# Layer 1 of a graph network on one core: three picked groups a turn, re-ordered steps, and a turned one-hot that is read with a stride

## What is computed

```
e_in     = concat(x[src], x[dst])                     # 200000 x 256
edge_new = relu(e_in @ We1 + be1) @ We2 + be2
agg      = segment_sum(edge_new, dst)                 # 6250 x 128
x        = layernorm(x + x + relu(concat(x, agg) @ Wn1 + bn1) @ Wn2 + bn2)
```

## Time and profile before

| | |
|---|---|
| median of three runs | 4093.22 us |
| profiled execution, its own time | 4090.99 us |
| its span | 4088.8 us |
| mean granted TensorE clock | 0.844 of 2.4 GHz |
| layer 1, first gather to the end | 2179.3 to 4088.8 us |
| PE, DVE, ACT, POOL busy, whole span | 2902.8, 2493.5, 2497.4, 2964.7 us |

### The profile page before, as it was taken

How to read it: one execution, slowest core, us unless ns; L and a number is a source line. 1 busy time by engine, 2 the same in 40 slices (tenths; PEclk the granted TensorE clock), 3 DMA queues, 4 the chain that set the end, 5 groups by cost and what they waited for, 6 DMA issues and landing times. The chain is left out here.

```text
span 4088.8 us, 90253 instructions
## 1 busy us (share of the span) xinstructions
PE 2902.8 (71%) x18890; PEld 2648.6 (65%) x18891; DVE 2493.5 (61%) x5568; ACT 2497.4 (61%) x10068; POOL 2964.7 (73%) x3137
## 2 busy tenths in 40 slices
PE   6888888888888788888865565655556565666656
PEld 4877777777777777777744555555556555555656
DVE  4877777777777777777765444444444555555544
ACT  3767777777777677777646555455555555555553
POOL 5777777777777777777536777777777777777775
PEclk8999999999999999999987777767767777777777
DMA  6333333333333333333234333333333333333332
GB/s 190 81 81 81 83 81 81 81 82 81 82 80 82 81 84 81 81 81 83 57 108 108 95 90 94 94 91 94 90 94 94 93 99 94 98 97 95 97 99 63
DMA packets 426429, 367.97 MB, mean 90 GB/s; under 512 B 276875, under 2 KB 355163, under 8 KB 426108
## 3 DMA queue, kind: packets, MB, share of 16 engines
q0 software_dynamic: 98240, 214.20, 20.4%
q1 hardware_dynamic: 316720, 143.31, 14.0%
q10 hardware_dynamic: 11214, 8.17, 0.7%
HBM read 343.89 MB, written 21.44 MB: 89 GB/s over the span
## 5 line engine op out<-in xcount | busy, mean ns | idle before, releaser
L724 POOL DMA_INDIRECT he<-h_table,src_i x1563 | 1480.7, 947 | 514.9 <-issue 504.3
L1744 POOL DMA_INDIRECT msg<-p_table,src x1507 | 1422.3, 944 | 467.1 <-issue 461.6
L1777 PE MATMUL p_sumT<-msg,hot 128*80 128x129 f32 x3136 | 595.7, 369 | 688.2 <-ACT sumT L1830 683.7
L1777 PEld LDWEIGHTS p_sumT<-msg,hot 128*80 128x80 f32 x3136 | 542.5, 215 | 725.4 <-issue 533.9
L1622 ACT COPY picked<-hT 128x1 f32 x7168 | 759.9, 187 | 412.4 <-issue 398.3
L1762 PE MATMUL p_edge<-r_win,hotT 80*128 80x128 f32 x3136 | 480.0, 312 | 59.7 <-DVE msg L1899 45.8
L763 PE MATMUL p_score<-qk_two,heT 128*128 128x160 f32 x1568 | 396.7, 336 | 165.4 <-ACT heT L873 163.4
L1762 PEld LDWEIGHTS p_edge<-r_win,hotT 80*128 80x128 f32 x3136 | 452.6, 227 | 63.7 <-issue 63.2
L1899 DVE TENSOR_TENSOR msg<-msg,p_edge 128x512 f32<-128x512 f32 x392 | 243.6, 662 | 377.5 <-DMA msg<-p_table,src 376.4
L765 PE MATMUL p_score<-qk_win,heT 128*128 128x80 f32 x3136 | 465.2, 273 | 0.0
L765 PEld LDWEIGHTS p_score<-qk_win,heT 128*128 128x128 f32 x3136 | 454.3, 200 | 0.0
(11 more groups left out here) (210 smaller groups left out, 4565.5 us busy)
## 6 DMA issues: line engine op xcount, KB each, us to landing
dst_row<-in_dst_dram SPq DMA_DIRECT2D x196, 320.0 KB
feat<-in_edge_attr_dram SPq DMA_DIRECT2D x196, 128.0 KB
he<-h_table,src_i POOLq DMA_INDIRECT x1563
msg<-p_table,src POOLq DMA_INDIRECT x1507
qk_win<-qk_table SPq DMA_DIRECT2D x196, 40.0 KB
qk_two<-qk_table SPq DMA_DIRECT2D x392, 20.0 KB
r_win<-r_table SPq DMA_DIRECT2D x196, 40.0 KB
qk_table<-qk SPq DMA_DIRECT2D x13, 512.0 KB
```

The lines of the kernel that those rows point to most:

```text
L724: e.indirect_dma_start(out=he[u][:, j, 2 * FE:2 * FE + ROW], out_offset=None, in_=h_table[:, :], in_offset=bass.IndirectOffsetOnAxis(ap=sr ...
L1744: e.indirect_dma_start(out=msg[u][:, j, 0:D], out_offset=None, in_=p_table[:, :], in_offset=bass.IndirectOffsetOnAxis(ap=src_i[u][:, j:j + ...
L1777: mm = e.matmul(p_sumT[:, :], hot_of(c)[:, j, :], msg[u][:, j, 0:D + 1], start=(j == 0), stop=(j == J - 1))
```

## The change

- `PICKED` is (5, 0, 3). Chunks 5 and 3 are picked by ACT, 128 columns each, chunk 0 by DVE (`tensor_copy`), 128 columns. `group_of` gives None for the two groups other than 5 in turn 0, so these chunks gather all eight columns there; from turn 1 on they are picked a turn ahead. `pick_first` is gone. `pick_step` spreads ACT's 256 columns over seven steps (37 each), DVE's 128 over the first five (26 each). The node numbers go to registers in up to 16 at a time.
- `hotT` keeps the order in which `dst_row` was loaded. Its one operation compares with the node's number plus the window's start, worked out once for all chunks (`node_b`), with no second operand. `column` gives TensorE every eighth number (every seventh in a picked chunk, after the first 128) as the weights.
- Steps: PE does `edges` of the next chunk, `turn_back` of the one before, `sums` of its own (before: `sums` of the one before, `turn_back` of two before, `edges` of the next). ACT does `copy_sums` of the one before, its relu, then the picks (before: picks, `copy_sums` of two before, relu). DVE does the one-hots of the next chunk, `add` of two before, the picks, `boths` (before: `boths`, then `add`). Below, the three `step` functions stand in this order.

```
-PICKED = (5, 1)
-BATCH = 8
-BY_ACT = P // BATCH
+PICKED = (5, 0, 3)
+BY_ACT = (P, 0, P)
+BY_DVE = tuple(P - n for n in BY_ACT)
+AT_ONCE = 16
...
-            hotTs = [sb(f"hotT{k}", [W, J, P], ctx=ctx) for k in range(2)]
+            hotTs = [sb(f"hotT{k}", [W, CH], ctx=ctx) for k in range(2)]
...
                     def group_of(c):
-                        return PICKED.index(c[1]) if at_first and c[1] in PICKED else None
+                        g = PICKED.index(c[1]) if at_first and c[1] in PICKED else None
+                        return None if g and isinstance(c[0], int) and c[0] == 0 else g
...
+                        start = first + (0 if of is BY_ACT else BY_ACT[g])
+                        parts = -(-n // AT_ONCE)
+                        ends = [start + n * k // parts for k in range(parts + 1)]
+                        for at, to in zip(ends, ends[1:]):
...
                             i, u = c
-                            if u == 2 and not (isinstance(i, int) and i == 0):
+                            if u == 0 and not (isinstance(i, int) and i == 0):
+                                load_picks(2, i)
+                            elif u == 3 and not (isinstance(i, int) and i == 0):
                                 load_picks(0, i)
-                            elif u == 5 and not (isinstance(i, int) and i == TURNS - 1):
+                            elif u == 4 and not (isinstance(i, int) and i == TURNS - 1):
                                 load_picks(1, i + 1)
...
+                        def column(c, j):
+                            flat = hotT_of(c)
+                            if is_last(c):
+                                return flat[:, j * P:(j + 1) * P]
+                            if group_of(c) is None:
+                                return flat[:, :].rearrange("w (p j) -> w j p", j=J)[:, j, :]
+                            if j == 0:
+                                return flat[:, 0:P]
+                            return flat[:, P:CH].rearrange("w (p j) -> w j p", j=J - 1)[:, j - 1, :]
...
                         def step(c):
-                            if not is_first(c):
-                                sums(shift(c, -1))
-                            if not is_first(c) and not is_first(shift(c, -1)):
-                                turn_back(shift(c, -2))
                             if not is_last(c):
                                 edges(shift(c, 1))
+                            if not is_first(c):
+                                turn_back(shift(c, -1))
+                            sums(c)
...
-                        def step(c):
+                        def step(c, k=None):
+                            if not is_first(c):
+                                copy_sums(shift(c, -1))
+                            relus(c)
+                            if k is not None and c[1] == 4:
+                                relu_hidden(e, k)
                             if at_first:
                                 pick_step(e, mybir.EngineType.Activation, e.copy, picked_act, c, BY_ACT)
-                            if not is_first(c) and not is_first(shift(c, -1)):
-                                copy_sums(shift(c, -2))
-                            relus(c)
...
+                            e.tensor_scalar(hotT_of(c)[:, :], dst_row[u][:, :], node_b[:, bass.ds(number(c), 1)], None,
+                                            ALU.is_equal).then_inc(hotT_done, 1)
...
                         def step(c):
                             if not is_last(c):
                                 hots(shift(c, 1))
-                            boths(c)
                             if not is_first(c) and not is_first(shift(c, -1)):
                                 add(shift(c, -2))
+                            if at_first:
+                                pick_step(e, mybir.EngineType.DVE, e.tensor_copy, picked_dve, c, BY_DVE)
+                            boths(c)
```

More of the change, by code:

```diff
@@ L1475, in gnn_kernel, with made @@
             picked_act = sem("picked_act")
-            def pick_number(g, turn):
-                return turn * len(PICKED) + (g - 1) % len(PICKED)
+            picked_dve = sem("picked_dve")
+            def made(of, g, turn):
+                each = sum(n > 0 for n in of)
+                upto = sum(n > 0 for n in of[0:g + 1])
+                return turn * each + (upto + each if g == 0 else upto)
             in_win_done = sem("in_win_done")
@@ L1620, in pick_columns @@
                                 skip_runtime_bounds_check_because="the source of an edge is the number of a node")
-                            for k in range(BATCH):
+                            for k in range(to - at):
                                 op = copy(picked[g][:, at + k:at + k + 1], x1T[:, bass.ds(nodes[k], 1)])
-                        if first + n == of:
+                        if first + n == of[g]:
                             op.then_inc(done, 1)
                     def pick_step(e, engine, copy, done, c, of):
-                        per = -(-len(PICKED) * of // SLOTS)
@@ L1638, in pick_first @@
-                    def pick_first(e, engine, copy, done, of):
-                        pick_columns(e, engine, copy, done, 1, 0, 0, of, of)
+                        per = -(-sum(of) // (SLOTS if of is BY_ACT else SLOTS - 2))
+                        at, end = c[1] * per, min((c[1] + 1) * per, sum(of))
+                        for g in range(len(of)):
+                            low = sum(of[0:g])
+                            first, n = max(at - low, 0), min(end - low, of[g]) - max(at - low, 0)
+                            turn = c[0] if g == 0 else c[0] + 1
+                            if n > 0 and not (isinstance(turn, int) and turn == TURNS):
+                                pick_columns(e, engine, copy, done, g, turn, first, n, of)
@@ L1659, in load_picks @@
                             if not isinstance(turn, int) or turn > 0:
-                                before = val(e, pick_number(g, turn) - len(PICKED) + 1)
-                                e.wait_ge(picked_act, before)
-                                e.sem_inc(passed, 1)
+                                for done, of in ((picked_act, BY_ACT), (picked_dve, BY_DVE)):
+                                    if of[g]:
+                                        e.wait_ge(done, val(e, made(of, g, turn - 1)))
+                                        e.sem_inc(passed, 1)
                             at = val(e, (turn * SLOTS + PICKED[g]) * CH)
@@ L1713, in _ @@
                         if at_first:
-                            for g in (1, 0):
-                                load_picks(g, 0)
+                            load_picks(0, 0)
                         for u in range(1, SLOTS):
@@ L1933, in step_grouped @@
                                 normal(e, k)
+                        e.tensor_scalar(node_b[:, :], start_b[0:W, :], node_c[:, 0:1], None, ALU.add).then_inc(fixed, 1)
+                        e.wait_ge(fixed, val(e, FIXED + 1 + r))
                         hots((0, 0))
                         if at_first:
+                            e.sem_inc(picked_dve, sum(n > 0 for n in BY_DVE))
                             e.sem_inc(y_done, 1)
```

57 lines of the change are left out of this document (20 added, 37 removed).

## The result

The changed kernel took 4568.52 us (median of 4 runs, 4564.85 to 4571.53) against 4095.76 (4 runs): a ratio of 1.1156 [1.1137, 1.1175]. It is slower by 11.6%, where 4062 and a gain of 0.8% were forecast. Its profiled execution took 4566.30 us with a span of 4564.6, that is 475.8 us more than the span of before.

What follows compares the result with a forecast made beforehand. POOL's queue of layer 1 gathers was taken as the bound: first gather 2179.3, plus 1847.9 to the last, plus 29.1 less 1.5 to the end, plus 5 for POOL, 2.2 around the span: 4062 us, range 4050 to 4096.

Steps and rivals of the forecast that it cites:

- Picks on ACT: ACT's 256 picked columns a turn: 0.162 us each with loads, 41 us a turn; larger batches at worst the same time.
- Picks on DVE: DVE's new 128 columns a turn, ahead of boths: 0.162 us each (0.06 to 0.24), 20.7 us a turn, 0 on the path.
- Rival D: DVE becomes the bound above 0.288 us a column; at 0.35 a turn is 74 us, some 4280 us; chance 0.04.
- Order of the steps: New step order on PE, ACT and DVE: hidden by POOL in steady state, 1.5 us won at the end (0 to 2.4).
- POOL beside DVE: New DVE work from SBUF to SBUF beside POOL's gathers: costs 5 us, bounds 0 and 27 us.
- rival B: The gathers get longer: 22 ns a gather eats the whole gain, 4091 us; chance 0.11.
- Rival C: A gather stands still while DVE runs a one-hot: 188 us minus 34, 4245 us; chance 0.03.
- Fewer gathers: POOL's gathers in layer 1 fall from 1507 to 1481, 26 less at 1.2486 us: 32.5 us off the path.
- The turned one-hot: DVE's one-hot falls from 2.08 us a chunk to 1.27 (lower end half of that); 0 on the path.
- TensorE reads it strided: TensorE's 16 strided weight loads a chunk take 1.61 times as long, 1.41 us more; 0 on the path under POOL.

Runs made afterwards that it cites:

- a1: The changed kernel with each batch of node numbers starting at a column that is a multiple of four: 4108.17 us, ratio 1.0017 to the kernel before.
- b1: The kernel before with its list of picks shifted by one number, so no batch of eight starts at a multiple of four: 4974.53 us, ratio 1.2132.
- a2: The changed kernel with DVE's add after boths again, batches still unaligned: 4334.59 us, ratio 1.0572 to the kernel before.
- a7: The changed kernel with batches starting at multiples of four and the turned one-hot's second operand in PSUM, still contiguous: 4111.61 us, ratio 1.0039 to the kernel before.
- a8: The changed kernel with batches at multiples of four, the one-hot's second operand in PSUM and DVE's add after boths: 4058.98 us, ratio 0.9909 to the kernel before.
- c3: a8 with the old order of steps on TensorE and ACT: 4230.62 us, ratio 1.0328 to the kernel before.
- c1: a8 with the old layout of the turned one-hot (DVE strided, TensorE's weights contiguous): 4060.04 us, ratio 0.9901 to the kernel before.
- b3: The kernel before with strided weights alone (one-hot contiguous, its second operand in PSUM): 4139.31 us, ratio 1.0107.
- b2: The kernel before with only the new one-hot from SBUF to SBUF and the strided weights: 4154.72 us, ratio 1.0145.

## Why the prediction was wrong

**The steps that failed first are "Picks on ACT" and "Picks on DVE".** They took 0.162 us a column on both engines and said of larger batches "at worst the same time". Measured: 0.240 and 0.290. The price of a register load was scaled with its length from one row of eight numbers; that the row held only batches from multiples of eight was not seen, and the change splits 37 columns of ACT's step in three and DVE's 26 in two. The upper end for DVE, 0.24, rested on the same row. Undoing this alone (a1) brings 4568 to 4108, and doing it alone (b1) brings 4101 to 4975. With aligned batches, the column costs 0.143 and 0.193: the form of the term was right.

**Rival D named half of the place, and was mis-sized.** It had a chance of 0.04, from 0.288 us a column on, and at 0.35 a turn of 74 us and 4280 us. DVE measured 0.290 with the ring and 0.252 without it (a2). Without the ring the turn is (4263.0 - 2185.5) / 28 = 74.2 us and the time 4335, but it is ACT that sets it there, the engine whose batches the prediction held to be harmless. In the kernel after the turn is 82.8 us, and that needs a second cause.

**"Order of the steps" failed in its one sentence on DVE.** "DVE the add before boths" was called hidden by POOL. What counted was not when DVE has time, but what it waits for there: the turned sums, which the new order puts behind the edges, which wait for boths. So an add that nobody needs soon closes a ring through both engines, with the picks inside it. It waited 423.2 us (a2: 50.7), and even with short loads and quick gathers the ring costs 53 us (a7 against a8). The other half of that step was mis-sized to the good side: of TensorE's and ACT's new order the prediction saw 1.5 us (0 to 2.4) at the end. With three groups and strided weights it is worth some 170 us (c3 against a8). From the last gather to the end a8 needs 29.1 - 25.9 = 3.2 us less than before; the timeline of a8 shows the last sums right behind the last relu, where they came 2.40 us late before:

```profile
4031.97 1.06 ACT L1841 ACTIVATE msg<-msg 128x1024 f32<-128x1024 f32 x1
...
4033.08 1.99 PE L1799 MATMUL p_sumT<-msg,hot 128*80 128x129 f32 x16 [0.53 <-ACT msg L1841]
```

**"POOL beside DVE" was mis-sized.** 5 us were taken, 27 was the upper end, and 22 ns a gather was the point where it eats the gain (rival B). In a1 it is 974 - 944 = 30 ns, 44 us over 1481 gathers, so the aligned kernel gained nothing. The row taken for it had four operations of an eighth of the size, and the gather that began among them lost 0.07 us. A single operation of 0.75 us holds a gather for up to half a microsecond, and it comes every chunk. Rival C, a gather that stands still while DVE runs a one-hot, was the right mechanism with too high a price: a gather is held only where it and the one-hot meet in certain stretches of each other, and the mean loss is 30 ns times 1481 / 196 gathers a chunk, 0.23 us, not 0.96.

**Right were** "Fewer gathers" (1481, and a8's pitch of (4028.0 - 2178.6) / 1480 = 1.2496 us against 1.2486); "The turned one-hot" as a time of DVE (0.77 us in the kernel after, 1.27 in a7 and a8; 0.64 to 1.27 forecast); and "TensorE reads it strided" as to its price, hidden in the new order (c1 as fast as a8), though b3 shows that in the old order the same loads cost 41 us. Its factor was met by luck: 747.0 / 452.6 = 1.65 against the 1.61 taken from DVE, but that is a mean over two clock levels, at which it is about 2 and 1.1, and from c1 to a8 it is 742.8 / 543.6 = 1.37. So the gain of 0.8% was there to be had, and what hid it were three things the sum held at nothing or nearly so.

What stays open: how much of c3's loss is ACT's order and how much TensorE's was not tried apart, and neither was whether the one-hot of a7 lets gathers pass for its operation or for its operand in PSUM.

## What to carry to other kernels

When a change alters the size of a batch, ask where each batch starts, and take the price of a load only from rows with the same start. When a wait is moved on an engine, follow it round: who must run for it, and whether that one waits for something behind it on the same engine; such a ring appears in no busy share. And a mean over many instructions can hide that a few are half as long again: look at the maximum, and at which operation beside them is new.

## What the runs showed of the hardware

- A register load of 8 to 16 numbers was quick only from a column that is a multiple of four. From such columns 8 numbers took 0.546 us, 12 numbers 0.79 and 13 numbers 1.03 on ACT: some 0.24 us for each four, and as much for a number left over. From others 8 numbers took 1.75, 12 numbers 2.6 and 13 numbers 2.83: some 0.22 us for each number (before, after, b1). Whether the column in the tile decides or the address was not tried.
- A `tensor_scalar` of 80x1024 from SBUF to SBUF takes 0.74 us, and where it meets a gather one of the two is often held: gathers took up to 1.47 us instead of 0.94 and one-hots up to 0.99 (after, b2). Gathers that began within a one-hot, or 0.1 to 0.5 us before one, lost time. The `scalar_tensor_tensor` form with a second operand in PSUM takes 1.27 us and lets gathers pass (a7: at most 1043 ns). One-column copies from SBUF to SBUF, 3456 of them, leave the gathers at 945 ns (a8).
- Sixteen weight loads that take 128 numbers 32 bytes apart keep TensorE's load path busy for 3.91 us at a granted clock of 1.00 and 3.83 at 0.50 (a8); contiguous ones for 1.86 and 3.49 (c1). The Trainium skill's "SBUF — State Buffer", section "Door 1: The DMA port swizzle", says that such reads pay a penalty and gives no size; in these rows it is large at the upper clock level and small at the lower one.
